# A four-layer graph network on one core: first gathering in two fp32r passes, large-count blocks found from the edge list, root product of layer two moved ahead

## The reference, cut to what matters

```
def rgcn_gate_layer(x, row, col, edge_type, basis, att, gate_w, root, bias):
    w = einsum('rb,bio->rio', att, basis)          # two 512x512 matrices from 30 basis matrices
    msg_r = sigmoid(x[col] @ gate_w[r])[:, None] * x[col] @ w[r]
    msg = where(edge_type == 0, msg_0, msg_1)
    return segment_sum(msg, row) + x @ root + bias
h = relu(rgcn_gate_layer(x, ..., basis1, att1, gate_w1, root1, bias1))
out = rgcn_gate_layer(h, ..., basis2, att2, gate_w2, root2, bias2)
```

## Time and profile before

| | |
|---|---|
| runs | 1156.43, 1159.91, 1161.3 us |
| profiled execution, its own time | 1161.15 us |
| its span in the trace | 1159.4 us |
| busy in the span | TensorE 94%, weight load 52%, VectorE 72%, ScalarE 48%, GpSimd 48% |
| mean granted TensorE clock | 0.985 of full |
| moved by DMA | 172.66 MB, 149 GB/s |
| first block (sort to tables) | 0 to about 462 us, barrier, next block from 466.6 us |

### The profile page before, as it was taken

The page is one execution under the profiler, slowest core; times in us unless marked ns, Lnnn a source line. Parts: engine busy times, 40 slices in busy tenths (PEclk is TensorE's granted clock), DMA queues, the critical chain, the costliest instruction groups (busy, mean ns, idle before and its releaser), DMA issues. The chain is left out here.

```text
span 1159.4 us, 15448 instructions
## 1 busy us (share of the span) xinstructions
PE 1086.1 (94%) x4410; PEld 607.0 (52%) x4442; DVE 835.8 (72%) x1852; ACT 558.3 (48%) x978; POOL 559.3 (48%) x518
## 2 busy tenths in 40 slices
PE   3989888899999989899999999999999999999997
PEld 1564222344557453655565565555555557446664
DVE  5694677769755153688788788788888867849997
ACT  0221321310332221477777777777777744116663
POOL 1960112233433330667876666666666300027774
PEclk9988989999999999899999999999999999999999
DMA  7995997657211005595554454445454010026665
GB/s 283 341 404 212 360 400 264 231 184 233 84 48 46 13 14 194 132 259 111 114 110 92 101 98 95 100 95 97 98 98 88 1 55 23 9 93 197 203 206 173
DMA packets 60182, 172.66 MB, mean 149 GB/s; under 512 B 12645, under 2 KB 13189, under 8 KB 52552
## 3 DMA queue, kind: packets, MB, share of 16 engines
q0 software_dynamic: 31536, 72.01, 26.6%
q1 hardware_dynamic: 28568, 99.66, 23.4%
HBM read 159.65 MB, written 11.98 MB: 148 GB/s over the span
## 5 line engine op out<-in xcount | busy, mean ns | idle before, releaser
L1664 PE MATMUL PS<-wide,hidT 128*128 128x512 f32 x672 | 302.1, 592 | 2.2 <-DVE hidT L1540 0.4
L705 POOL DMA_INDIRECT rec_scratch<-rec_src,slot_row x84 | 102.5, 1220 | 252.8 <-DMA rec_scratch<-rec_src,slot_row 208.2
L1664 PEld LDWEIGHTS PS<-wide,hidT 128*128 128x128 f32 x672 | 128.6, 191 | 122.8 <-issue 120.5
L1482 POOL DMA_INDIRECT pair_sum<-table_j,counts_rec x84 | 136.7, 1627 | 27.3 <-issue 25.3
L1598 ACT ACTIVATE wide<-PS 128x512 f32<-128x512 f32 x168 | 100.5, 598 | 99.6 <-PE PS L1648 63.5
L1801 POOL DMA_INDIRECT u_space<-table_j,wide x87 | 86.1, 990 | 108.7 <-DMA table_j<-agg_space 81.8
L1474 POOL DMA_INDIRECT pair_sum<-table_i,counts_rec x84 | 89.5, 1066 | 98.9 <-PE PS L1648 59.5
L1603 ACT ACTIVATE wide<-wide,two 128x512 f32<-128x512 f32 x168 | 120.9, 720 | 6.2 <-DVE wide L1533 6.2
L1533 DVE SCALAR_TENSOR_TENSOR wide<-wide 128x512 f32<-128x512 f32 x168 | 116.4, 693 | 5.8
L1491 POOL DMA_INDIRECT rec_scratch<-rec_src,slot_row x84 | 89.5, 1066 | 40.9 <-issue 21.6
L1608 ACT ACTIVATE wide<-wide 128x512 f32<-128x512 f32 x168 | 105.8, 630 | 5.3
(11 more groups left out here) (325 smaller groups left out, 1884.9 us busy)
## 6 DMA issues: line engine op xcount, KB each, us to landing
pieces<-basis_rows SPq DMA_DIRECT2D x56, 1024.0 KB, 7.5
ring<-basis_low SPq DMA_DIRECT2D x30, 256.0 KB, 6.4
w_scratch<-pieces SPq DMA_DIRECT2D x112, 32.0 KB
counts_rec<-rec_scratch SPq DMA_DIRECT2D x1, 2856.0 KB, 9.8
rec_scratch<-rec_src,slot_row POOLq DMA_INDIRECT x168, 2.3
root<-L_gnn_root SPq DMA_DIRECT2D x2, 1024.0 KB, 8.0
rows_in<-in_rows_in SPq DMA_DIRECT2D x2, 1024.0 KB, 13.9
w_rel<-w_scratch SPq DMA_DIRECT2D x1, 2048.0 KB, 11.6
```

Of the source, the lines that this page charges most:

```text
L705: nc.gpsimd.indirect_dma_start(out=rec3_dram, out_offset=bass.IndirectOffsetOnAxis(ap=slot_row[:, 1, t:t + 1], axis=0), in_=rec, in_offset ...
L1482: nc.gpsimd.indirect_dma_start(out=pair_sum[:, t % GOT3, :], out_offset=None, in_=tables[0][1], in_offset=bass.IndirectOffsetOnAxis(ap=idx ...
L1664: m = nc.tensor.matmul(o, hidT[:, t % 2, k * P:(k + 1) * P], w2[:, k, :], start=False, stop=(k == KT - 1), skip_group_check=True)
```

## The change

1. **First gathering in two passes.** `y_first` now lies in ten consecutive slots of `pieces` (still with the four slots of `root` among them); ScalarE makes ten high parts `first_hi` (in the space of `packed`, `ones_part` and the one-hots), VectorE ten low parts `first_lo` in place, and ScalarE rounds the ten count rows (`counts_rounded`) among them, not in step two. The gathering is then 100 fp32r matmuls and four for the rests of heavy blocks. One matmul for each chunk comes first, then the rests, then 19 for each chunk. VectorE does the two `split_block` and all ten `first_low` behind `unpack` and ahead of the bias and `sum2`.
2. **Heavy blocks from the edge list.** During the sort, VectorE copies the group membership of sources and destinations (`both_kinds`, 3 instructions), TensorE multiplies them (`pair_sums`, 7 matmuls in bf16), VectorE keeps what belongs together (`sums_of_groups`, 4), TensorE adds up (`block_sums`, 5 small fp32 matmuls), VectorE copies (`sums_of_blocks`, 3) and runs `heavy_blocks` twice (now 19 instructions each). `largest`, `mark_heavy`, `heavy` and the two copies of marks are gone. `with_loops` adds the rests back to two blocks, since it now reads rounded counts.
3. **Order.** The root product of step two stands ahead of the gates and products Y1. `SUM2_BEFORE_H1` is (6, 6, 6, 6, 6). `records()` moves from count `t` = 6 to sort `e` = 40. The four numbers that TensorE reads for the rests stand ahead of the late products Y0. SyncE's queue is not changed.

The core of the diff:

```diff
-            SUM2_BEFORE_H1 = (16, 11, 11, 11, 11)
+            SUM2_BEFORE_H1 = (6, 6, 6, 6, 6)
...
-                def gathered_first(c):
-                    for m_ in range(NT):
-                        if c == 0:
-                            pe.wait_ge(sem("counts"), 2 * NT + m_ + 1)
-                        for r in range(2):
-                            m = nc.tensor.matmul(PS[:, c, :], counts[r][:, m_, c * P:(c + 1) * P], y_first(r, m_),
+                FIRST_TERMS = [(m_, r, part) for m_ in range(NT) for r in range(2) for part in (first_hi, first_lo)]
+
+                def gathered_first(c, terms):
+                    for m_, r, part in terms:
+                        pe.wait_ge(sem("counts_short"), 2 * m_ + r + 1)
+                        pe.wait_ge(sem("first_lo" if part is first_lo else "first_hi"), 2 * m_ + r + 1)
+                        m = nc.tensor.matmul(PS[:, c, :], counts_short[r][:, m_, c * P:(c + 1) * P], part[:, first_at(r, m_), :],
...
+                pe.wait_ge(sem("heavy_at"), 2)
+                rest_chunk = [rest_numbers(j, 8, NT - 1) for j in range(2)]
+                rest_first = [rest_numbers(j, 12, 2 * NT - 1) for j in range(2)]
                 early_late = Y0_LATE[0]
...
-                for c in range(NT):
-                    gathered_first(c)
+                pe.wait_ge(sem("rests"), 2)
+                for c in range(NT):
+                    gathered_first(c, FIRST_TERMS[:1])
+                pe.wait_ge(sem("first_hi"), 2 * NT)
+                pe.wait_ge(sem("first_lo"), 2 * NT)
+                for j in range(2):
+                    rest(rests[:, j, :], rest_chunk[j], (first_hi, first_lo), rest_first[j])
+                for c in range(NT):
+                    gathered_first(c, FIRST_TERMS[1:]).then_inc(sem("o0_mm"), 1)
                     if c:
                         pe.wait_ge(sem("h1"), c)
                         turn_rows(c - 1, turn(("T1", c - 1), alone))
 
                 for c in range(NT):
+                    if c == 0:
+                        pe.wait_ge(sem("root_in"), 32)
+                        for d in range(NT):
+                            if d == 1:
+                                pe.wait_ge(sem("h1"), NT)
+                                turn_rows(NT - 1, turn(("T1", NT - 1), alone))
+                            pe.wait_ge(sem("side_ev"), side["T1", d] + 1)
+                            root_rows(d)
                     gates(1, (c,), turn(("G1", c), alone))
...
-                pe.wait_ge(sem("root_in"), 32)
-                for c in range(NT):
-                    root_rows(c)
                 pe.wait_ge(sem("y_lo"), 2 * NT)
...
                 for c in range(NT):
                     unpack(2, c)
+                split_block(0)
+                split_block(1)
+                for n in range(2 * NT):
+                    first_low(n)
...
+                    if n == FIRST_HIGH_AT:
+                        for i in range(n + 1):
+                            first_high(i)
+                    if n > FIRST_HIGH_AT:
+                        first_high(n)
+                        for _ in range(ROUNDED_PER[n]):
+                            counts_rounded(*rounded.pop(0))
```

More of the change, by code:

```diff
@@ L196, in gnn_stack @@
             y_more = pieces[:, 4 * RING1:4 * RING1 + 2, :]
-            stage = pieces[:, 4 * RING1 + 2:4 * RING1 + 2 + STAGE, :]
+            root = pieces[:, 4 * RING1 + 2:4 * RING1 + 2 + KT, :]
+            stage = pieces[:, SLOTS - STAGE:SLOTS, :]
             ring2 = sb("ring2", [P, RING2, LOW * D], F32, early)
-            root = sb("root", [P, KT, D], F32, early)
             rows_in = sb("rows_in", [P, 4, D], F32, early)
+            packed_at = nc.sbuf_base
             packed = sb("packed", [P, NT, NP], F32, early)
@@ L237, in gnn_stack @@
             group_id = part(10)
[L238 removed]
+            values = part(11)
             by_chunk = part(12).rearrange("p (j t) -> p j t", j=4)
@@ L434, in gathered, with pair_sums, block_sums @@
                     m.then_inc(sem("o1_mm"), 1)
[L436 to L440, removed]
+                def pair_sums():
+                    pe.wait_ge(sem("src_group"), 3)
+                    for g in range(ET // SUM_TILES):
+                        tiles = slice(SUM_TILES * g, SUM_TILES * (g + 1))
+                        m = nc.tensor.matmul(PS[0:SUM_ROWS, SUMS_BANK, 0:2 * SUM_ROWS].rearrange("p (q k t) -> p q k t", q=2, k=NT),
+                                             dst_group[:, g, :, :].rearrange("p k t -> p (k t)"), src_group[:, :, :, tiles],
+                                             start=(g == 0), stop=(g == ET // SUM_TILES - 1), skip_group_check=True)
+                    m.then_inc(sem("pair_sums"), 1)
+                def block_sums():
+                    pe.wait_ge(sem("group_sums"), 4)
+                    for k in range(NT):
+                        m = nc.tensor.matmul(PS[0:1, SUMS_BANK, 2 * NT * k:2 * NT * (k + 1)], own_group[:, k:k + 1], group_sums,
+                                             start=(k == 0), stop=True, skip_group_check=True)
+                    m.then_inc(sem("block_sums"), 1)
                 def rest_numbers(j, at, bound):
@@ L474, in _ @@
                         gates(0, range(NT), early_side("G0"))
+                    if e == PAIR_SUMS_AT:
+                        pair_sums()
+                    if e == BLOCK_SUMS_AT:
+                        block_sums()
                     if e in R0_SORT:
@@ L1189, in _ @@
+                    for j in range(2):
+                        b = dve.value_load(heavy_at[0:1, 16 + j:17 + j], min_val=0, max_val=NT * NT - 1)
+                        block = blocks[1][:, bass.ds(b, 1), :].rearrange("p b n -> p (b n)")
+                        nc.vector.tensor_tensor(block, block, rests[:, j, :].bitcast(F32), ALU.add).then_inc(sem("all_edges"), 1)
+                        dve.wait_ge(sem("all_edges"), 2 + NT + j)
                 for c in range(NT):
@@ L1357, in _ @@
                         nc.scalar.copy(y_hi[:, NT * r + c, :], y_rows[:, NT * r + c, :]).then_inc(sem("y_hi"), 1)
-                    if c in HEAVY_AT:
-                        g = HEAVY_AT.index(c)
-                        keep_product(("heavy", g), found_of[g], rows=slice(0, 1))
-                for r in range(2):
-                    for m in range(NT):
-                        act.wait_ge(sem("rests"), 2)
-                        nc.scalar.copy(counts_short[r][:, m, :], counts[r][:, m, :]).then_inc(sem("counts_short"), 1)
                 act.wait_ge(sem("deg"), 1)
```

255 lines of the change are left out of this document (155 added, 100 removed).

## The result

The changed kernel takes **1176.58 us** (median of 4 runs, 1171.29 to 1179.21) against 1160.61 us for the kernel before (median of 4): ratio 1.0145, 95% interval 1.0116 to 1.0174. It is slower, by about 16 us. The forecast was 1172 with a range of 1154 to 1180.

A forecast was written before the change was run, and what follows sets the result against it. TensorE was taken to bound the kernel, as long as VectorE and transfers keep up. Terms -17.3 + 22.7 + 2.2 + 2.9 + 1.5 - 0.2 = +11.8 us, so 1173.0 profiled, 1172 median; range 1154 to 1180.

The forecast's parts named there:

- Sort stage, number reads and gathering: TensorE to the first gathering's end: sort stage 0, reads 1.0 late, gathering done at 267.5 instead of 284.79, minus 17.3 us.
- rival B: Sort stage: delays of 2.5 us fill a stall, TensorE's clock isn't lowered; gives back up to 6.5, 1165; chance 0.09.
- The number reads: Four reads ahead of the late products Y0 hold TensorE 0 (queue full) to 2.4 us; taken as 1.0.
- the last low part: First gathering: after five fp32r matmuls TensorE waits for VectorE's last low part until 243.1, idle 0.9 us.
- Rival C: First gathering: each fp32r matmul takes 0.429, so it ends at 287.4; +15, 1175; chance 0.10 together with D.
- The stall: Ahead of the root product, TensorE stands from 267.5 until root lands at 290.2, behind SyncE's low pieces: plus 22.7 us.
- The clock behind the stall: After the idle time TensorE runs some 4.4 us at its lower clock level: plus 2.2 us, bound 0 to 6.5.
- End of step two: Behind Y1, no longer covered by the root product: low part, reads, rests plus 2.9 us; clock drop plus 1.5.
- The records and VectorE: Records packed earlier in the sort: GpSimd's first scatter near 83, last near 423, worth nothing in time.
- Rival A: SyncE's queue: root issued at 267.5, lands 273.5; stall 6.0, sum -4.9, or 1151 without clock terms; chance 0.14.
- Rival D: Behind the gathering: lower clock level for 13 us and root at 292; +18, 1178; chance 0.10 together with C.

The follow-up runs named there:

- the moved transfer: Changed kernel with the second root matrix issued in SyncE's queue ahead of low piece b = 22, not behind all low pieces: 1158.57 us, ratio 0.9981 to the kernel before.
- the filler: Changed kernel with 23 fp32 matmuls, whose result nobody reads, on TensorE in the stall for root: 1170.93 us, ratio 1.0105 to the kernel before.

## Why the prediction was right, and where its terms were off

The forecast was +11.8 us for the profiled execution and 1172 for the median; it was +10.1, and 1176.58, inside the range. The median's own difference is +16.0, 4 us over the forecast, in executions without a trace. The mechanism was the one forecast, at each of its places; the sizes differ by term.

**Sort stage, number reads and gathering (forecast 1.0 late, then minus 17.3; measured minus 18.5).** The count began at 103.32 us and not at 105.62. That isn't shown to be the change's doing, or rival B: in nine kernels of the experiments that have the changed kernel's sort stage it began anywhere between 100.69 and 105.44, and at 104.23 with the records early alone. The number reads cost more than forecast: the idle time is 2.50 us where I took 1.0, with some work in the queue in mind; my bound of 2.4 for an empty queue was the right value. Ahead of the reads stand only the count's last matmuls, 0.22 to 0.38 us each, and they are over at 204.21. The wait for the last low part was 0.83 (forecast 0.9), the gathering's pace as in the earlier trace rows. Rival C is out.

**The stall (forecast 22.7; measured 21.42).** VectorE's last low part was over at 241.6, not 243.1, so SyncE came to root at 277.63, not 279.6; it landed 10.2 us later, at 287.8, where I had 10.6. From the first of the three transfers to the last landing it is 11.2 us; my sum from the earlier trace rows had 11.7. The root of the earlier trace rows that I called a lone one was not: SyncE issued two more transfers of 1 MB 0.4 and 1.0 us behind it. It was the first of three, so the 6.0 is the time of one with nothing of its size ahead, as the 6.5 of the moved transfer is. An estimate by the Trainium skill, "DMA: Bandwidth & Descriptors" (Anatomy of one DMA), whose fit is for transfers that GpSimd issues while these are SyncE's, makes 9.2 of the 11.2, which is 2.0 short. The time of landing that it gave, 287.7, came out by a start that was forecast too late.

**The clock behind the stall (forecast 2.2; measured 1.6 in the profile).** 5.22 us against 3.6. The bound of 6.5 was never reached in a trace, but the filler took 5.6 us off the median. So the profile of one execution, the fastest of four, may show this term too small; no trace of a slower one is there.

**End of step two (forecast 2.9 and 1.5; measured 4.3).** The gap is 2.93 us, the rests 2.11 and the next 60 matmuls 0.7 slower. Only the split was off.

**What I had not listed:** the clock falls a third time in the GCN product, 1.7 us with the rest product before it. The same pause by number reads stands in the kernel before, where the clock stayed up. It makes up for more than half of what the other terms came out lower (some 3 us), so part of the agreement of the sum is luck.

**The records and VectorE.** First scatter at 83.29 us (forecast 83), last one at 426.05 (423), worth nothing, as forecast and as the experiment alone shows.

**Rival A** stands as a mechanism: with its landing forced, the kernel is no loss. With the clock terms I had put it at 4.9 us under the kernel before, and the distance is 3.1 shorter. The price without them, 1151, was too good: 1158.6, since the stall of 6.15 still brought the clock down (5.91 us for eight records, 0.57 granted between 275 and 280). Rival D is out: root landed at 287.8, not 292. The experiment with the root product behind Y1 adds what the prediction had only in its first paragraph ("as long as VectorE keeps up"): without the moved product the sums alone would have eaten the gain.

## What to carry to other kernels

When a product is moved to the front, move its operand's transfer too, past everything in the queue that waits for a slower engine: here the place of the one transfer was 14 us in the traces and 18 in the medians. Before a stage is made faster, look at what else ends with it; here 18.5 us off TensorE only uncovered VectorE's sums, and it took other TensorE work to fill their time. Put scalar reads on an engine's sequencer behind a long product: four of them cost TensorE 2.5 us behind the short matmuls of the count and nothing that shows behind products of 3.7 us.

## What the runs showed of the hardware that I had not expected

Reads of numbers by TensorE's sequencer cost some 0.5 to 0.75 us each with only short matmuls ahead of them (0.96 to 1.07 for two in the GCN, 2.48 to 3.01 for four), and nothing visible when two stand behind a product of 3.7 us. The pause ahead of a product doesn't tell by itself whether the clock falls. In the GCN product, 130 us behind the stall, the 24 matmuls took 5.61 to 5.64 us in the kernels before, with early records, with the filler and with the root product behind Y1, and 6.5 to 7.2 in those with the root product first and no filler, at idle times before them that were the same within 0.15 us. A long stall earlier doesn't tell it either: the kernel with the root product behind Y1 had one of 19.71 us and is among the fast ones. What decides it stays open. And the clock of the sort stage differed between executions of kernels with the same instructions there, which moves the start of the gathering by some us (238.67 with the filler, 246.84 with the root product behind Y1): a difference of 3 us between two profiles has to be counted from a common mark.
